# Dynamic filters on one core: pairs of squared filter tiles summed by TensorE alone, its sums of one chunk placed between the taps of the next

## The chip, the cores and the metric

One Trainium2 chip, and of it one core. The metric is the device time of one execution in microseconds (us); lower is better. The kernel before takes 20082.18 us, the median of three runs (20081.55 to 20100.58).

## What is computed

A network of four layers on images of 4 x 64 x 128 x 128, float32. Only the fourth layer, the dynamic filters, is touched:

```python
h = x                                   # x here: the group-normalised input
for _ in range(5):                      # STEPS
    t = gelu(einsum('oc,bchw->bohw', W1, h) + b1)          # exact gelu
    k = einsum('oc,bchw->bohw', W2, t) + b2                # 64 channels x 9 taps
    k = k.reshape(B, C, 9, H, W)
    k = k / (norm(k, axis=2) + 1e-6)                       # over the nine taps
    y = sum(patches(h) * k, axis=2)                        # 3x3 neighbourhood
    h = h + alpha * y
out = x_raw + h
```

So each pixel of each channel makes its own filter of nine taps, which is divided by the root of the sum of its nine squares, and applied to the pixel's neighbours.

## The kernel before, in words

The layers run one after the other. The last one is `dynamic_filters` (L1721 to L2077). The padded image of one batch stands in `df_h`, in both halves of the 128 partitions (64 channels each), one half for the even and one for the odd rows of a chunk. A **chunk** is 8 rows, a tile of 128 partitions x 512 float32. Four chunks are a **group** (c = 0 to 3), four groups an image; 4 batches x 5 steps x 4 groups make 80 groups (`q`) and 320 chunks (`n`).

For one chunk:

- TensorE makes the hidden layer, `hid` (L1823, matmul L1830) with the whole array. ScalarE turns it to `df_t` by a gelu (L1892).
- TensorE makes nine tiles of filters, `tap` (L1832). Taps 0 to 5 (L1840) use 64 rows of the array each, the upper half for even and the lower for odd taps, and can run two at a time. Taps 6 to 8 (L1843) use the whole array. All go through five banks of PSUM (`df_pk`, `BANKS`): tap j waits until square j - 5 has been taken.
- VectorE multiplies each tile of filters, with its bias, by the shifted image (L2056) into `df_pr`; ScalarE squares the same tile (L1902) into `df_sq`, after the product. Both rings hold 15 tiles.
- GpSimd adds squares 0, 2, 4 and 1, 3, 5 (four `add`s, L1954), products 6 and 7 (`singles`, L1959) and squares 6, 7, 8 (two more `add`s).
- TensorE sums products 0 to 5 over the two halves (`sums`, L1851, with the stacked identities `df_pair`), adds product 8 (L1854), both into `df_py`, and sums the two tiles of added squares into `df_pn` (L1861). These matmuls write 64 partitions each, and use 64 columns of the array each, so two can run at a time.
- VectorE joins these with GpSimd's parts (`join`, L1998 and L2001).

The order on TensorE is written out (L1865 to L1876): taps 0 to 5 of chunk n, all sums of chunk n - 1, the hidden matmul of n + 1, taps 6 to 8 of n. On VectorE the join of chunk n - 1 follows product 5 of chunk n (L2063), and on ScalarE the gelu of n + 1 follows square 5.

For a group that is complete, on top: ScalarE takes root, logarithm and exponential of the sums of squares, two instructions each, with three swaps of its function table and a fourth back to the gelu (L1905 to L1921), placed after squares 7 and 8 of chunk 0 and 0 to 3 of chunk 1 of the next group. GpSimd scales (L1965), VectorE checks (L2006) and refines (L2013). Two groups later, in chunk 0, VectorE updates the image (`update`, L2022, after products 0 to 3), or in the last step of a batch writes the output tile (L2028) and adds the raw input (`residual`, L2036, after products 4 to 7); that last case is 16 of the 80 groups. SP's queue copies updated rows between the halves (L1790, L1791) and stores.

Of the kernel before, what the change touches and what calls it, by code (L numbers as in the profile page):

```python
# [18 lines left out]
KK = 9  # L19
# [12 lines left out]
class Steps:  # L32
# [5 lines left out]
    def add(self, ins):  # L38

        ins.then_inc(self.sem, 1)  # L40
        self.n += 1
# [1679 lines left out]
def dynamic_filters(env, ins, x3, out):  # L1721
# [3 lines left out]
    nc = env.nc  # L1725
    CH, GR, R = 4, 4, 8
    N = R // 2 * W
    BANKS, RING = 5, 15
    GROUPS = [(b, step, g) for b in range(B) for step in range(STEPS) for g in range(GR)]
    Q = len(GROUPS)  # L1730
    NC = Q * CH
# [14 lines left out]
    with ExitStack() as m:  # L1746
# [73 lines left out]
        @block.tensor  # L1820
        def _(pe):
            def hid(n):
                b, step, g = GROUPS[n // CH]  # L1823
                if n:
                    pe.wait_ge(active, n)
                if step:
                    pe.wait_ge(moved, CH * updates(b, step, g))
                else:
                    pe.wait_ge(normed, b * GR + g + 1)
                nc.tensor.matmul(p1[:, :], w1[:, :], centre(n), start=True, stop=True).then_inc(hidden, 1)  # L1830

            def tap(n, k):  # L1832
                j = KK * n + k
                if k == 0:
                    pe.wait_ge(active, n + 1)
                if j >= BANKS:
                    pe.wait_ge(squared, j - BANKS + 1)
                if k < 6:
                    p = slice(64 * (k % 2), 64 * (k % 2) + 64)
                    nc.tensor.matmul(pk[:, j % BANKS, :], wp[p, k // 2, :], t[p, n % 2, :], start=True, stop=True,  # L1840
                                     tile_position=(64 * (k % 2), 0)).then_inc(tapped, 1)
                else:
                    nc.tensor.matmul(pk[:, j % BANKS, :], ws[:, k - 6, :], t[:, n % 2, :], start=True, stop=True).then_inc(tapped, 1)  # L1843

            def sums(n):
                pe.wait_ge(product, KK * n + KK)
                if n:
                    pe.wait_ge(yjoined, n)
                for k in range(6):
                    s = k % 2  # L1850
                    nc.tensor.matmul(py[64 * s:64 * s + 64, :], pair[:, :], pr[:, (KK * n + k) % RING, :], start=(k < 2), stop=False,  # L1851
                                     tile_position=(0, 64 * s))
                for s in range(2):
                    last = nc.tensor.matmul(py[64 * s:64 * s + 64, :], env.ident[:, 64 * s:64 * s + 64],  # L1854
                                            pr[:, (KK * n + 8) % RING, :], start=False, stop=True, tile_position=(0, 64 * s))
                last.then_inc(ysummed, 1)
                pe.wait_ge(nadded, 6 * n + 4)
                if n:
                    pe.wait_ge(njoined, n)
                for s in range(2):  # L1860
                    last = nc.tensor.matmul(pn[64 * s:64 * s + 64, :], pair[:, :], sq[:, (KK * n + s) % RING, :], start=True, stop=True,  # L1861
                                            tile_position=(0, 64 * s))
                last.then_inc(nsummed, 1)

            pe.wait_ge(w_in, 64)  # L1865
            hid(0)
            for n in range(NC):
                for k in range(6):
                    tap(n, k)
                if n:  # L1870
                    sums(n - 1)
                if n + 1 < NC:
                    hid(n + 1)
                for k in range(6, KK):
                    tap(n, k)
            sums(NC - 1)  # L1876

        @block.scalar
        def _(act):
# [14 lines left out]
            def square(n, k):  # L1894
                j = KK * n + k
                if k == 0 and n >= 2:
                    act.wait_ge(njoined, n - 1)
                if k == 6 and n:
                    act.wait_ge(nsummed, n)
                act.wait_ge(product, j + 1)  # L1900
                bias = V_B2 + (k // 2 if k < 6 else k - 3)
                nc.scalar.activation(sq[:, j % RING, :], pk[:, j % BANKS, :], ACT.Square, bias=env.vecs[:, bias:bias + 1]  # L1902
                                     ).then_inc(squared, 1)

            def root(q, i):  # L1905
                act.wait_ge(njoined, CH * q + 2 * i + 2)
                n = nr[:, q % 2, 2 * i:2 * i + 2, :]
                nc.scalar.activation(n, n, ACT.Sqrt).then_inc(rooted, 1)  # L1908
# [18 lines left out]
            for n in range(NC):  # L1927
                q, c = n // CH, n % CH
                for k in range(KK):
                    square(n, k)  # L1930
                    if k == 5 and n + 1 < NC:
                        gelu(n + 1)
                    if q and (c, k) in ((0, 7), (0, 8)):
                        root(q - 1, k - 7)
                    if q and (c, k) in ((1, 0), (1, 1)):
                        log(q - 1, k)
                    if q and (c, k) in ((1, 2), (1, 3)):
                        seed(q - 1, k - 2)
                    if q >= 2 and (c, k) == (3, 2):
                        b, step, g = GROUPS[q - 2]  # L1940
                        if step == STEPS - 1 and b + 1 < B:
                            norm(b + 1, g)
# [4 lines left out]
        @block.gpsimd  # L1947
        def _(pool):
            def add(n, into, other, earlier=0):
                pool.wait_ge(squared, KK * n + other + 1)  # L1950
                if earlier:
                    pool.wait_ge(nadded, 6 * n + earlier)
                a = sq[:, (KK * n + into) % RING, :]
                nc.gpsimd.tensor_tensor(a, a, sq[:, (KK * n + other) % RING, :], ALU.add).then_inc(nadded, 1)  # L1954

            def singles(n):
                pool.wait_ge(product, KK * n + 8)
                a = pr[:, (KK * n + 6) % RING, :]
                nc.gpsimd.tensor_tensor(a, a, pr[:, (KK * n + 7) % RING, :], ALU.add).then_inc(sadded, 1)  # L1959

            def scale(q, i):
                pool.wait_ge(seeded, 2 * q + i // 2 + 1)
                pool.wait_ge(yjoined, CH * q + i + 1)
                y = yr[:, q % 2, i, :]
                nc.gpsimd.tensor_tensor(y, y, inv[:, i, :], ALU.mult).then_inc(scaled, 1)  # L1965

            for n in range(NC):
                q, c = n // CH, n % CH
                add(n, 0, 2)
                add(n, 1, 3)  # L1970
                if q and c == 2:
                    scale(q - 1, 1)
                add(n, 0, 4, 1)
                add(n, 1, 5, 2)
                if q and c == 2:
                    scale(q - 1, 2)
                singles(n)
                add(n, 6, 7)
                if q and c == 2:
                    scale(q - 1, 3)  # L1980
                add(n, 6, 8, 5)
                if q and c == 1:
                    scale(q - 1, 0)
            for i in range(CH):
                scale(Q - 1, i)

        @block.vector
        def _(dve):
# [2 lines left out]
            nc.vector.memset(h[64:128, H:H + 1, 1:W + 1], 0.0).then_inc(link, 1)  # L1991
            dve.wait_ge(link, 3)

            def join(n):
                q, c = n // CH, n % CH
                dve.wait_ge(ysummed, n + 1)
                dve.wait_ge(sadded, n + 1)
                nc.vector.tensor_tensor(yr[:, q % 2, c, :], py[:, :], pr[:, (KK * n + 6) % RING, :], ALU.add).then_inc(yjoined, 1)  # L1998
                dve.wait_ge(nsummed, n + 1)
                dve.wait_ge(nadded, 6 * n + 6)  # L2000
                nc.vector.tensor_tensor(nr[:, q % 2, c, :], pn[:, :], sq[:, (KK * n + 6) % RING, :], ALU.add).then_inc(njoined, 1)  # L2001

            def check(q, i):
# [31 lines left out]
                dve.wait_ge(stepout, o + 1)  # L2035
                nc.vector.tensor_tensor(yo[:, i, :], yo[:, i, :], ro[:, i, :], ALU.add).then_inc(o_out, 1)  # L2036

            CHECK = {(1, 6): 0, (1, 8): 1, (2, 1): 2, (2, 3): 3}
            REFINE = {(2, 5): 0, (2, 7): 1, (3, 1): 2, (3, 3): 3}
            dve.wait_ge(env.loaded, env.loads)  # L2040
            nc.vector.tensor_scalar(alpha[:, :], env.vecs[:, V_ALPHA:V_ALPHA + 1], -1.0, None, ALU.mult).then_inc(negated, 1)
            dve.wait_ge(negated, 1)
            for n in range(NC):
                q, c = n // CH, n % CH
                b, step, g = GROUPS[q]
                for k in range(KK):
# [4 lines left out]
                            dve.wait_ge(copied[g - 1], 32 * (b * STEPS + step + 1))  # L2051
                    if k == 6 and c == CH - 1 and g + 1 < GR:
                        dve.wait_ge(copied[g + 1], 32 * (b * STEPS + step + 1))
                    dve.wait_ge(tapped, j + 1)
                    bias = V_B2 + (k // 2 if k < 6 else k - 3)
                    nc.vector.scalar_tensor_tensor(out=rows(pr[:, j % RING, :]), in0=rows(pk[:, j % BANKS, :]),  # L2056
# [3 lines left out]
                        update(q - 2, k)  # L2060
                    if q >= 2 and c == 0 and 4 <= k < 4 + CH and GROUPS[q - 2][1] == STEPS - 1:
                        residual(q - 2, k - 4)
                    if k == 5 and n:  # L2063
                        join(n - 1)
                    if q and (c, k) in CHECK:
                        check(q - 1, CHECK[c, k])
                    if q and (c, k) in REFINE:
                        refine(q - 1, REFINE[c, k])
            join(NC - 1)
            for i in range(CH):  # L2070
                check(Q - 1, i)
                refine(Q - 1, i)
# [149 lines left out]
```

## Time and profile before

| | |
|---|---|
| median of three runs | 20082.18 us |
| the profiled execution | 20080.48 us |
| its span, first to last instruction | 20078.7 us |
| mean granted clock of TensorE, share of full speed | 0.736 |
| TensorE, VectorE, GpSimd, ScalarE busy, of the span | 62%, 52%, 47%, 28% |
| instructions of TensorE's matmuls | 73490 |

The last layer takes the last 4.5 ms. A float32 matmul of 512 columns leaves two records in the trace, one for each half of its passes. "Idle before" in a row is the time for which the engine had stood before it, and "<-" names what ended it. PE is TensorE's matmuls, PEld its weight loads, which can lie under a matmul. A row that ends in xN merges N instructions in a row; its length is from the first one's start to the last one's end.

### The profile page before, as it was taken

To read this page: it belongs to the slowest core of one execution; us is meant where nothing else is said; L and a number is where in the kernel's file an instruction comes from. 1 tells how busy PE (TensorE), PEld (TensorE's weight loads), DVE (VectorE), ACT (ScalarE), POOL (GpSimd) and SP (SyncE) were. 2 spreads that over 40 slices of the span, in tenths; PEclk is the share of its full clock that TensorE was granted. 3 is DMA by queue.
4 is the path that set the end of the run, shared out by engine and by line. 5 is a ranking of instruction groups with operands and counts; after the bars stand their busy time and mean duration, and the time that the engine had idled before them with its cause. 6 is when DMAs were issued, how large, how long until landed. Compare 5 with 4: busy or idle time off the path is not lost. (4 is left out here: it accounts for less than half of the span.)

```text
span 20078.7 us, 217701 instructions
## 1 busy us (share of the span) xinstructions
PE 12353.6 (62%) x73490; PEld 6114.7 (30%) x73490; DVE 10535.6 (52%) x14652; ACT 5526.4 (28%) x7765; POOL 9453.1 (47%) x8026
## 2 busy tenths in 40 slices
PE   5553699999999202333333333333358899999998
PEld 2551366666666101111111111111112333333332
DVE  4557544444444333443443444344422788888887
ACT  1114333333333000000000000000010666666666
POOL 0113100000000106886887788688800787878787
PEclk9999856656666556666666666666679999999999
DMA  4104222222222494335334433533342112121201
GB/s 94 33 21 102 55 38 36 37 38 36 36 37 38 135 195 111 95 95 131 95 95 107 120 95 95 131 96 95 95 86 58 33 22 42 21 42 22 42 19 30
DMA packets 1399772, 1408.47 MB, mean 70 GB/s; under 512 B 771709, under 2 KB 1116045, under 8 KB 1383565
## 3 DMA queue, kind: packets, MB, share of 16 engines
q1 hardware_dynamic: 1106892, 742.84, 18.5%
q0 software_dynamic: 221184, 604.27, 10.4%
q10 hardware_dynamic: 70976, 50.83, 0.8%
q8 instruction: 567, 9.29, 0.2%
q14 instruction: 153, 1.25, 0.0%
HBM read 1036.74 MB, written 276.84 MB: 65 GB/s over the span
## 5 line engine op out<-in xcount | busy, mean ns | idle before, releaser
L1359 POOL DMA_INDIRECT dc_g<-corners,dc_idx x4608 | 5253.7, 1140 | 1326.0 <-issue 1260.9
L1954 POOL TENSOR_TENSOR df_sq<-df_sq 128x512 f32<-128x512 f32 x1920 | 2713.0, 1427 | 1866.6 <-ACT df_sq L1902 1839.5
L1432 PE MATMUL dc_ps<-ident,dc_s 128*128 128x128 f32 x2560 | 674.0, 428 | 4296.9 <-DVE dc_s L1523 4294.8
L1079 POOL TENSOR_TENSOR nz_vp<-nz_vp,nz_den 128x2048 f32<-128x2048 f32 x16 | 105.8, 6610 | 4814.7 <-DMA nz_den<-den_d 4814.7
L1515 DVE TENSOR_TENSOR dc_g<-dc_g,dc_wt 128x2304 f32<-128x2304 f32 x512 | 1308.6, 2556 | 2001.0 <-DMA dc_g<-corners,dc_idx 2000.9
L1902 ACT ACTIVATE df_sq<-df_pk,vecs 128x512 f32<-128x512 f32 x2880 | 1921.1, 685 | 1326.0 <-DVE df_pr L2056 1309.2
L2056 DVE SCALAR_TENSOR_TENSOR df_pr<-df_pk,vecs,df_h 128x512 f32<-128x512 f32 x2880 | 2047.6, 741 | 407.1 <-PE df_pk L1840 264.5
L1432 PEld LDWEIGHTS dc_ps<-ident,dc_s 128*128 128x128 f32 x2560 | 472.0, 218 | 4480.6 <-DVE dc_s L1523 3352.1
L1392 ACT ACTIVATE dc_st<-dc_ps 128x512 f32<-128x512 f32 x640 | 327.0, 607 | 4934.2 <-PE dc_ps L1432 4934.2
L1840 PE MATMUL df_pk<-df_t,df_wp 64*128 64x512 f32 x3840 | 1389.8, 642 | 364.7 <-ACT df_sq L1902 302.1
L916 DVE TENSOR_REDUCE at_mx<-at_pt 128x4 f32<-128x512 f32 x1024 | 707.8, 691 | 1605.4 <-PE at_pt L779 1605.4
L839 PE MATMUL at_prr<-at_a,at_rel 48*128 48x64 bf16 x8192 | 1029.5, 284 | 58.7 <-DMA at_k<-y 58.7
L779 PE MATMUL at_pt<-ident,at_x 128*128 128x128 f32 x4096 | 1053.1, 407 | 0.4 <-DVE at_x L925 0.3
L1851 PE MATMUL df_py<-df_pr,df_pair 128*64 128x512 f32 x3840 | 1025.9, 675 | 1.1 <-DVE df_pr L2056 1.1
L907 DVE SCALAR_TENSOR_TENSOR at_x<-at_pq,hconst,at_x 128x512 f32<-128x512 f32 x1024 | 715.5, 745 | 567.5 <-PE at_pq L759 402.9
L1438 PE MATMUL dc_po<-dc_st,dc_wd 128*64 128x512 f32 x1280 | 864.8, 843 | 92.1 <-ACT dc_st L1392 92.1
L839 PEld LDWEIGHTS at_prr<-at_a,at_rel 48*128 48x128 bf16 x8192 | 825.4, 119 | 307.9 <-ACT at_x L942 171.4
L1843 PE MATMUL df_pk<-df_t,df_ws 128*128 128x512 f32 x1920 | 875.4, 592 | 0.0
L1840 PEld LDWEIGHTS df_pk<-df_t,df_wp 64*128 64x128 f32 x3840 | 495.7, 188 | 1212.6 <-ACT df_sq L1902 816.7
L1234 PE MATMUL cv_po<-cv_xp,cv_w 128*64 x1536 | 682.0, 601 | 275.9 <-DVE cv_xo L1709 168.4
L942 ACT ACTIVATE at_x<-at_prr 128x512 f32<-128x512 f32 x1024 | 610.0, 596 | 869.7 <-PE at_prr L839 869.7
L925 DVE TENSOR_TENSOR at_x<-at_pt,at_x 128x512 f32<-128x512 f32 x1024 | 680.2, 686 | 158.9 <-PE at_pt L797 152.6
(271 smaller groups left out, 19428.1 us busy)
## 6 DMA issues: line engine op xcount, KB each, us to landing
df_h<-df_h SPq DMA_DIRECT2D x160, 512.0 KB, 7.1
dc_g<-corners,dc_idx POOLq DMA_INDIRECT x4608, 2.8
corners<-dc_xt SPq DMA_DIRECT2D x16, 4160.0 KB, 41.5
dc_xp<-x SPq DMA_DIRECT2D x8, 4096.0 KB, 40.8
cv_xp<-x SPq DMA_DIRECT2D x8, 4096.0 KB, 50.0
y<-sp_p SPq DMA_DIRECT2D x128, 192.0 KB, 2.8
y<-sp_p SPq DMA_DIRECT2D x64, 384.0 KB, 4.3
at_a<-y SPq DMA_DIRECT2D x64, 384.0 KB
```

The lines of the kernel that those rows point to most:

```text
L779: last = nc.tensor.transpose(ptt[:, t % 2, 128 * e:128 * e + 128], X[:, s, nh, :], env.ident[:, :])
L839: last = nc.tensor.matmul(prr[:, r % 2, 64 * i:64 * i + 64], rel[:, 127 - p:255 - p], a[0:48, s, :, :].rearrange("c h (n p) -> c (h n) p", ...
L1359: nc.gpsimd.indirect_dma_start(gt[:, r, k, :, :].rearrange("p a c -> p (a c)"), None, image, bass.IndirectOffsetOnAxis(ap=idx[:, s, r, k:k ...
L1432: i = nc.tensor.transpose(ps[:, j, 128 * r:128 * r + 128], sm[:, r % 2, 128 * j:128 * j + 128], env.ident[:, :])
L1438: i = nc.tensor.matmul(po[:, :], wd[:, j, :], stt[:, j, :], start=(j == 0), stop=(j == 4))
L1515: c.run(nc.vector.tensor_tensor(q, q, w, ALU.mult))
L1840: nc.tensor.matmul(pk[:, j % BANKS, :], wp[p, k // 2, :], t[p, n % 2, :], start=True, stop=True, tile_position=(64 * (k % 2), 0)).then_inc ...
L1843: nc.tensor.matmul(pk[:, j % BANKS, :], ws[:, k - 6, :], t[:, n % 2, :], start=True, stop=True).then_inc(tapped, 1)
L1851: nc.tensor.matmul(py[64 * s:64 * s + 64, :], pair[:, :], pr[:, (KK * n + k) % RING, :], start=(k < 2), stop=False, tile_position=(0, 64 * s))
L1902: nc.scalar.activation(sq[:, j % RING, :], pk[:, j % BANKS, :], ACT.Square, bias=env.vecs[:, bias:bias + 1]).then_inc(squared, 1)
L1954: nc.gpsimd.tensor_tensor(a, a, sq[:, (KK * n + other) % RING, :], ALU.add).then_inc(nadded, 1)
L2056: nc.vector.scalar_tensor_tensor(out=rows(pr[:, j % RING, :]), in0=rows(pk[:, j % BANKS, :]), scalar=env.vecs[:, bias:bias + 1], in1=shift ...
```

## The change

GpSimd no longer adds squares 0 to 5; it keeps `singles` and the two adds of squares 6 to 8, in another order (`singles` first). TensorE sums all six squares of the pairs itself, three pairs of matmuls instead of one, accumulated in `df_pn`. `sums` is split into `products(n, i)`, i = 0 to 3, and `squares(n, i)`, i = 0 to 2. In chunk n the squares of n - 1 stand after taps 1, 3 and 5, and the products of n - 1 after taps 6, 7, 8 and once more behind. The rings of products and squares hold 18 tiles, two chunks, and VectorE gets waits before it writes over a product of chunk n - 2. The join is split: products of n - 2 after product 1 of chunk n, squares of n - 1 after product 7. ScalarE loses its wait for the sums of squares, and root, logarithm and exponential are placed one square later; the checks and refinements of VectorE move a little later too.

```diff
-    BANKS, RING = 5, 15
+    BANKS, RING = 5, 18
+    ADDS = 2
...
-            def sums(n):
...
+            def products(n, i):
+                pe.wait_ge(product, KK * n + (2 * i + 2 if i < 3 else KK))
+                if i == 0 and n:
                     pe.wait_ge(yjoined, n)
...
+                for s in range(2):
+                    half = py[64 * s:64 * s + 64, :]
+                    if i < 3:
+                        last = nc.tensor.matmul(half, pair[:, :], pr[:, (KK * n + 2 * i + s) % RING, :], start=(i == 0), stop=False,
+                                                tile_position=(0, 64 * s))
+                    else:
+                        last = nc.tensor.matmul(half, env.ident[:, 64 * s:64 * s + 64], pr[:, (KK * n + 8) % RING, :],
+                                                start=False, stop=True, tile_position=(0, 64 * s))
                 last.then_inc(ysummed, 1)
...
+            def squares(n, i):
+                if i == 0:
+                    pe.wait_ge(squared, KK * n + 2)
+                    if n:
+                        pe.wait_ge(njoined, n)
+                else:
+                    pe.wait_ge(squared, KK * n + 2 * i + 2)
+                for s in range(2):
+                    k = 2 * i + s
+                    last = nc.tensor.matmul(pn[64 * s:64 * s + 64, :], pair[:, :], sq[:, (KK * n + k) % RING, :],
+                                            start=(i == 0), stop=(i == 2), tile_position=(0, 64 * s))
+                if i == 2:
+                    last.then_inc(nsummed, 1)
...
             for n in range(NC):
-                for k in range(6):
-                    tap(n, k)
-                if n:
-                    sums(n - 1)
+                for i in range(3):
+                    tap(n, 2 * i)
+                    tap(n, 2 * i + 1)
+                    if n:
+                        squares(n - 1, i)
                 if n + 1 < NC:
                     hid(n + 1)
                 for k in range(6, KK):
                     tap(n, k)
-            sums(NC - 1)
+                    if n:
+                        products(n - 1, k - 6)
+                if n:
+                    products(n - 1, 3)
...
-                if k == 6 and n:
-                    act.wait_ge(nsummed, n)
...
+                    if q and (c, k) in ((0, 8), (1, 0)):
+                        root(q - 1, c)
+                    if q and (c, k) in ((1, 1), (1, 2)):
+                        log(q - 1, k - 1)
+                    if q and (c, k) in ((1, 3), (1, 4)):
+                        seed(q - 1, k - 3)
...
-                add(n, 0, 2)
-                add(n, 1, 3)
                 if q and c == 2:
                     scale(q - 1, 1)
-                add(n, 0, 4, 1)
-                add(n, 1, 5, 2)
+                singles(n)
                 if q and c == 2:
                     scale(q - 1, 2)
-                singles(n)
                 add(n, 6, 7)
...
-                add(n, 6, 8, 5)
+                add(n, 6, 8, 1)
...
-            CHECK = {(1, 6): 0, (1, 8): 1, (2, 1): 2, (2, 3): 3}
-            REFINE = {(2, 5): 0, (2, 7): 1, (3, 1): 2, (3, 3): 3}
+            CHECK = {(1, 7): 0, (2, 0): 1, (2, 2): 2, (2, 4): 3}
+            REFINE = {(2, 6): 0, (2, 8): 1, (3, 2): 2, (3, 4): 3}
...
+                    if n >= 2 and k in (0, 2, 4, 8):
+                        dve.wait_ge(ysummed, 4 * (n - 2) + min(k // 2, 3) + 1)
+                    if n >= 2 and k == 6:
+                        dve.wait_ge(yjoined, n - 1)
...
-                    if k == 5 and n:
-                        join(n - 1)
+                    if k == 1 and n >= 2:
+                        join_products(n - 2)
+                    if k == 7 and n:
+                        join_squares(n - 1)
```

## Rows read from the trace of the kernel before

**Rows 1.** The page: busy time of each engine, and the second costliest group

```profile
PE 12353.6 (62%) x73490; PEld 6114.7 (30%) x73490; DVE 10535.6 (52%) x14652; ACT 5526.4 (28%) x7765; POOL 9453.1 (47%) x8026
...
L1954 POOL TENSOR_TENSOR df_sq<-df_sq 128x512 f32<-128x512 f32 x1920 | 2713.0, 1427 | 1866.6 <-ACT df_sq L1902 1839.5
```

**Rows 2.** The view of the image's tile: line, engine, count: ns min/median/max, first and last start

```profile
L2056 DVE SCALAR_TENSOR_TENSOR df_pr<-df_pk,vecs,df_h x2880: 729/739/753, 15597.4 to 20027.2; 128x512 f32<-128x512 f32 x192
...
L2022 DVE SCALAR_TENSOR_TENSOR df_h<-df_y,df_alpha,df_h x256: 731/1240/1705, 15696.6 to 19863.6; 128x512 f32<-128x512 f32 x128
```

**Rows 3.** Waits of the whole run: engine, waited for whom: us, times, longest

```profile
POOL df_sq L1954 <- ACT df_sq L1902: 1839.5, 487, 1027.0
...
PEld df_pk L1840 <- ACT df_sq L1902: 816.7, 817, 2.7
```

**Rows 4.** Timeline of TensorE over a group: start us, us, what, records, idle before

```profile
17031.00 2.80 PE L1851 MATMUL df_py<-df_pr,df_pair 128*64 128x512 f32 x12
17033.63 1.03 PE L1854 MATMUL df_py<-df_pr,ident 128*64 128x512 f32 x4
17034.49 1.03 PE L1861 MATMUL df_pn<-df_sq,df_pair 128*64 128x512 f32 x4
17035.45 1.13 PE L1830 MATMUL df_p<-df_h,df_w 128*128 128x512 f32 x2
17036.42 2.73 PE L1843 MATMUL df_pk<-df_t,df_ws 128*128 128x512 f32 x6
17039.08 2.32 PE L1840 MATMUL df_pk<-df_t,df_wp 64*128 64x512 f32 x8
17043.22 1.12 PE L1840 MATMUL df_pk<-df_t,df_wp 64*128 64x512 f32 x2 [1.82 <-ACT df_sq L1902]
17044.75 1.12 PE L1840 MATMUL df_pk<-df_t,df_wp 64*128 64x512 f32 x2 [0.40 <-ACT df_sq L1902]
17045.80 4.49 PE L1851 MATMUL df_py<-df_pr,df_pair 128*64 128x512 f32 x12
...
17051.94 1.13 PE L1830 MATMUL df_p<-df_h,df_w 128*128 128x512 f32 x2
...
17056.45 2.86 PE L1840 MATMUL df_pk<-df_t,df_wp 64*128 64x512 f32 x10 [0.80 <-ACT df_t L1892]
...
17085.76 0.65 PE L1851 MATMUL df_py<-df_pr,df_pair 128*64 128x512 f32 x2
```

**Rows 5.** Views of the lines of hidden and single taps' matmuls, ns min/median/max

```profile
L1830 PE MATMUL df_p<-df_h,df_w x640: 592/698/1193, 15576.8 to 20012.0; 128*128 128x512 f32 x160
...
L1843 PE MATMUL df_pk<-df_t,df_ws x1920: 590/592/697, 15601.0 to 20026.3; 128*128 128x512 f32 x192
```

**Rows 6.** Timeline: weight load of a hidden matmul after sums

```profile
17120.35 0.30 PEld L1830 LDWEIGHTS df_p<-df_h,df_w 128*128 128x128 f32 x2 [0.81 <-issue]
```

**Rows 7.** Timelines: a lone tap and its product; three products and their squares

```profile
17097.98 1.12 PE L1840 MATMUL df_pk<-df_t,df_wp 64*128 64x512 f32 x2 [1.82 <-ACT df_sq L1902]
...
17099.14 0.75 DVE L2056 SCALAR_TENSOR_TENSOR df_pr<-df_pk,vecs,df_h 128x512 f32<-128x512 f32 x1 [1.35 <-PE df_pk L1840]
...
17125.23 2.05 DVE L2056 SCALAR_TENSOR_TENSOR df_pr<-df_pk,vecs,df_h 128x512 f32<-128x512 f32 x3
...
17126.00 2.00 ACT L1902 ACTIVATE df_sq<-df_pk,vecs 128x512 f32<-128x512 f32 x3 [1.29 <-DVE df_pr L2056]
```

**Rows 8.** Timeline of ScalarE: ends of its run of table functions

```profile
17095.00 1.28 ACT L1908 ACT_TABLE_LOAD   x1
...
17110.46 0.69 ACT L1892 ACTIVATE df_t<-df_p,vecs 128x512 f32<-128x512 f32 x1
```

**Rows 9.** Groups of VectorE in the stage: busy us, mean ns, idle before

```profile
L2036 DVE TENSOR_TENSOR df_o<-df_o,df_raw 128x512 f32<-128x512 f32 x64 | 54.5, 859 | 2.3 <-DMA df_raw<-x 2.3
```

**Rows 10.** Stretches: length, busy of PE, PEld, DVE, ACT, POOL, granted clock, DMA

```profile
17101.40:17104.80 3.40, 3.40 (x12) 0.99 (x10) 0.01 (x1) 3.38 (x5) 0.62 (x1) 0.62 0.00 0
```

More of the change, by code:

```diff
@@ L1843, in tap @@
                     nc.tensor.matmul(pk[:, j % BANKS, :], ws[:, k - 6, :], t[:, n % 2, :], start=True, stop=True).then_inc(tapped, 1)
-            def sums(n):
-                pe.wait_ge(product, KK * n + KK)
-                if n:
+            def products(n, i):
+                pe.wait_ge(product, KK * n + (2 * i + 2 if i < 3 else KK))
+                if i == 0 and n:
                     pe.wait_ge(yjoined, n)
-                for k in range(6):
-                    s = k % 2
-                    nc.tensor.matmul(py[64 * s:64 * s + 64, :], pair[:, :], pr[:, (KK * n + k) % RING, :], start=(k < 2), stop=False,
-                                     tile_position=(0, 64 * s))
@@ L1853, in sums @@
                 for s in range(2):
-                    last = nc.tensor.matmul(py[64 * s:64 * s + 64, :], env.ident[:, 64 * s:64 * s + 64],
-                                            pr[:, (KK * n + 8) % RING, :], start=False, stop=True, tile_position=(0, 64 * s))
-                last.then_inc(ysummed, 1)
-                pe.wait_ge(nadded, 6 * n + 4)
-                if n:
-                    pe.wait_ge(njoined, n)
-                for s in range(2):
-                    last = nc.tensor.matmul(pn[64 * s:64 * s + 64, :], pair[:, :], sq[:, (KK * n + s) % RING, :], start=True, stop=True,
-                                            tile_position=(0, 64 * s))
@@ L1863, in sums @@
-                last.then_inc(nsummed, 1)
+                    half = py[64 * s:64 * s + 64, :]
[5 more added lines that the diff above has]
+                                                start=False, stop=True, tile_position=(0, 64 * s))
@@ L1867, in _ @@
             for n in range(NC):
-                for k in range(6):
-                    tap(n, k)
-                if n:
-                    sums(n - 1)
+                for i in range(3):
[3 more added lines that the diff above has]
+                        squares(n - 1, i)
                 if n + 1 < NC:
@@ L1875, in _ @@
                     tap(n, k)
-            sums(NC - 1)
+                    if n:
+                        products(n - 1, k - 6)
+                if n:
+                    products(n - 1, 3)
+            for i in range(3):
+                squares(NC - 1, i)
+            for i in range(4):
+                products(NC - 1, i)
         @block.scalar
@@ L1932, in _ @@
                         gelu(n + 1)
[L1933 to L1938, printed above, removed]
+                    if q and (c, k) in ((0, 8), (1, 0)):
[4 more added lines that the diff above has]
+                        seed(q - 1, k - 3)
                     if q >= 2 and (c, k) == (3, 2):
@@ L1951, in add @@
                 if earlier:
-                    pool.wait_ge(nadded, 6 * n + earlier)
+                    pool.wait_ge(nadded, ADDS * n + earlier)
                 a = sq[:, (KK * n + into) % RING, :]
@@ L1992, in _, with join_products, join_squares @@
             dve.wait_ge(link, 3)
-            def join(n):
+            def join_products(n):
                 q, c = n // CH, n % CH
-                dve.wait_ge(ysummed, n + 1)
+                dve.wait_ge(ysummed, 4 * n + 4)
                 dve.wait_ge(sadded, n + 1)
                 nc.vector.tensor_tensor(yr[:, q % 2, c, :], py[:, :], pr[:, (KK * n + 6) % RING, :], ALU.add).then_inc(yjoined, 1)
+            def join_squares(n):
+                q, c = n // CH, n % CH
                 dve.wait_ge(nsummed, n + 1)
-                dve.wait_ge(nadded, 6 * n + 6)
+                dve.wait_ge(nadded, ADDS * n + ADDS)
                 nc.vector.tensor_tensor(nr[:, q % 2, c, :], pn[:, :], sq[:, (KK * n + 6) % RING, :], ALU.add).then_inc(njoined, 1)
@@ L2068, in _ @@
                         refine(q - 1, REFINE[c, k])
-            join(NC - 1)
+            join_products(NC - 2)
+            join_squares(NC - 1)
+            join_products(NC - 1)
             for i in range(CH):
```

## The prediction

> **What bounds the kernel now.** The page first: it gives each engine's busy time and names the costliest groups; GpSimd's additions of squares at L1954 stand second, 1920 of them at 1.43 us [rows 1]. Then the tile of the image: the 2880 products run from 15597.4 to 20027.2 us, 4430 us for 320 chunks of nine, 13.85 us a chunk [rows 2]. Only this stage is touched.
>
> Then the waits. GpSimd sat 1839.5 us waiting for ScalarE's squares, 1027.0 of them in one wait that began ahead of the stage, so 812 in it: it is ahead of its work; TensorE's weight loads sat 816.7 us until a square freed a bank of products' filters [rows 3]. So the additions that the change takes away are not what the stage waits for. What it waits for is a ring: tap, product, square, bank free, next tap.
>
> Then TensorE's own timeline over one group of four chunks, from the sums of one group's chunk 0 to the same place in the next: 17031.00 to 17085.76, 54.76 us [rows 4]. 80 such groups make 4381 us; the other 49 us are the 16 groups in which the residual is added too. Within it the reader is to see three things. (a) Where TensorE runs unhindered, every matmul costs two records 0.429 us apart, 0.858 us, and two taps on the two row halves, or two sums on the two column halves, share one such slot: the pair of sums at 17033.63 to 17034.49 is 0.86. I call 0.858 a slot. (b) One chunk in four is long: 17035.45 to 17051.94 from one hidden matmul to the next, 16.5 us, because ScalarE swaps tables and TensorE idles 1.82 and 0.40 us. (c) A slot that follows another partition of the array costs more.
>
> **What a change of partition costs.** From sums (column halves) to the hidden matmul (whole array): 17034.49 to 17035.45, 0.96, and then 0.97 to the first single tap, where slots are 0.86. Three single taps and the change to row halves: 17036.42 to 17039.08, 2.66 against 3 x 0.858 = 2.57 [rows 4]. The first record after such a change lasts 698 ns (median of the line) and not 592 [rows 5]: its weight load, two records of 0.30 us in all, starts only together with the matmul, 0.81 us after the previous one [rows 6], where otherwise it lies under the matmul before. So 0.09 of gap and 0.11 of unhidden load: 0.20 us into whole or row halves. Into the column halves a load has 64 columns: one tap and the change take 17044.75 to 17045.80 = 1.05, and of that 0.11 is the tap's own late load, 0.86 its slot, so the gap is 0.08 to 0.09; the three pairs after it at 17031.00 take 2.63 for 2.57, so 0.05 to 0.06 of load. 0.14 us.
>
> **The change, part by part.**
> TensorE before: 3 tap pairs, 3 single taps, the hidden matmul, 4 pairs for products, 1 for squares, 12 slots = 10.30 us, and 3 changes (0.14 + 0.20 + 0.20), 10.84 us of 13.85.
> TensorE after: 2 pairs of squares more, 14 slots = 12.01 us. The order is now tap pair, squares, tap pair, squares, tap pair, squares, hidden and tap 6, products, tap 7, products, tap 8, two pairs of products: 12 changes, 6 into column halves (0.84 to 0.85) and 6 into the others (1.20): 2.05 us. Sum **14.06 us a chunk**, already 0.21 over what a chunk takes now. All of it is on the path, since nothing can shorten TensorE's own queue.
> Waits inside it. In the steady state I find none: a bank is free again 1.16 (tap to product) + 0.77 (product to square) + 0.69 (square) = 2.6 us after its tap [rows 7], and five taps further on there are at least 4.1 us of TensorE's queue (two tap pairs and two pairs of squares with changes). VectorE in chunk 0: 9 products and 2 joins at 0.66 apart (three products in 2.05 us, one alone 0.74, [rows 2, 7]) and 4 updates at about 1.2 [rows 2]: product 8 may start 1.16 + 10 x 0.66 + 4 x 1.2 = 12.6 us after the first tap, and its tap is ready at 11.15 + 1.16 = 12.3. Chunk 2 with 3 checks and 2 refinements fills VectorE to some 13.5 of 14.06. Both just fit.
> ScalarE, the one stall left. Its run from the first table load to the end of the gelu is 17095.00 to 17111.15, 16.15 us without a gap [rows 8]. Root, logarithm and exponential move one square later, so one square of 0.6 less lies between: 15.6. It begins when the square of tap 8 of chunk 0 is done: tap 8's start + 2.6. The gelu ends at tap 8 + 18.2 and the first tap of chunk 2 needs it. TensorE would arrive there at tap 8 + 2.9 (its slot, two pairs, changes) + 14.06 = 17.0. Stall 1.3, taken as 1.35. Taps 5 to 8 of chunk 1 need squares that end before TensorE reaches them (tap 8: square 3, at about + 12 us against 13.9).
> A group: 4 x 14.06 + 1.35 = **57.6 us** against 54.76: 80 x 2.84 = +227 us.
> The 16 groups with residuals: four additions of 0.86 us [rows 9] lie ahead of product 8 of chunk 0 on VectorE, so the run of ScalarE starts later. Before, this costs 49/16 = 3.1 us a group. After, I take 2.5 (updates meet GpSimd less), but TensorE then idles near 4 us in one piece, and the clock should fall as it does today after 1.82 + 0.40 of idling: + 1.7. So 4.2 for 3.1: +16 us.
> GpSimd: 4 of 8 additions a chunk go. Their gain lies on VectorE: an update lasts 731 ns alone and 1240 at the median, while a product that reads PSUM stays at 739 [rows 2]. But VectorE is not what the next tap waits for, so I cost it at nothing; if TensorE were not the cover it would be worth up to 0.5 us for each of 12 operations a group. The joins' separate places, the ring of 18 and VectorE's five new waits: each waits for matmuls at least most of a chunk old, nothing. The wait of ScalarE for the sums of squares goes, nothing. DMAs: none moves, SP's queue sees the same updates. End of the stage: three pairs more before the last joins, less GpSimd work behind; within 2 us, -1 taken.
> The granted clock now falls once a group: sums that take 2.80 at full clock (2.4 GHz) take 4.49 at 17045.80, a clock of 0.62 over 17101.40 to 17104.80 in the next group, where 0.5 would be 1.2 GHz throughout [rows 4, 10]. These 1.7 us are inside the 54.76 of now. I take it that 1.35 us of idling once a group leaves the clock up: the 0.80 us at 17056.45 does, 1.82 + 0.40 doesn't [rows 4]. It is between them, and this is the widest uncertainty.
> Changes from column halves to row halves and from the whole array to column halves appear in no row of before. Bounds: nothing, or 0.20 and 0.14 as their mirror images. If nothing, 2 x 0.20 + 3 x 0.14 = 0.82 go, a chunk is 13.24, the stall grows to about 3.0 because ScalarE's run starts with VectorE's product 8 and not with the tap, and a group is 56.0: +99 us and so still slower. I take the mirror images. The Trainium skill, "TensorEngine Tiling (Array Packing)", section Key Properties, says that a change of tiling mode drains the engine, not merely a change of tile; by that all twelve are paid, and the sum would be the one above. The rows agree for the three kinds that occur.
>
> Sum: profiled execution 20080.5 (span 20078.7 and 1.8 around it) + 227 + 16 - 1 = 20322; the median of the runs shown is 1.7 above the profiled one. **20320 us.**
>
> **Rivals.**
> 1. The clock falls in every group. For: 1.35 us of idling is nearer to 1.82 than to nothing; against: it is one short piece, and elsewhere TensorE is full. 64 more groups x 1.7 = +109: **20430**.
> 2. No stall at the gelu (ScalarE's run shorter or earlier than I count) or the unseen changes cheap: 320 x 14.06 = 4499 against 4430, +70, or the +99 above: **20150 to 20190**.
> 3. Faster: the interleaved changes are hidden, since weight loads could be drawn ahead between waits. For: nothing in the rows except that the unseen kinds are unseen; against: all 320 hidden matmuls show it. Then TensorE needs 12.01 a chunk and VectorE with ScalarE set the time: product 8 of chunk 0 at about 10.6 with updates at 0.73, gelu 17.0 later, the next two chunks at 12: 27.7 + 24 = 51.8 a group, 80 x -3.0 = -235: **19845**. It decides once a change costs under 0.05 us. With VectorE not relieved, the group is 55.2 and the kernel the same within 40 us.
> 4. Nothing to see: the change is off the path altogether. It can't be for TensorE's order, so this is small: **20080**.
>
> **How the numbers follow.** Forecast 0.58, rival 1 0.22, rival 2 0.09, rival 3 0.06, rival 4 with the half-relieved case 0.05. 0.2% is 40 us, about what a measurement of this kernel tells from no change. Slower 0.58 + 0.22 + 0.09 = 0.89; faster 0.06; same 0.05. Range: 20130 (the low end of rival 2) to 20450 (rival 1 and 20 us); outside it lie 0.11 below and perhaps 0.08 above, for stalls of chunk 2 where VectorE just fits.
>
> **What would show it.** TensorE busy all but 1 to 2 us a group; hidden matmuls 14.0 to 14.1 us apart in chunks 2, 3 and 0, and some 15.4 for the one that holds the gelu's stall; first records after a change at 698 and 643 ns, 12 times a chunk; updates on VectorE at 0.73 to 1.1 us; GpSimd's busy share in the stage about halved; the clock full in groups without residual. Hidden matmuls 12 to 13 us apart would prove the price of a change wrong; long gaps before squares or products would show a wait that I missed.

## The result

The changed kernel takes 20282.06 us, the median of four runs (20270.30 to 20296.69), against 20081.86 us (four runs): ratio 1.0098, 95% interval 1.0081 to 1.0116. It is slower by 200 us; forecast was 240 us, 20320, in a range from 20130 to 20450. The profiled execution took 20271.4 us, its span is 20269.5, and 191 us of the difference to the span of before lie between the first and the last product of the stage: 4621.3 us for 4429.8 [rows 2].

The page and the view of the image's tile (columns as in [rows 1, 2]), changed kernel:

```profile
PE 12789.9 (63%) x76050; PEld 5870.8 (29%) x76050; DVE 10144.9 (50%) x14652; ACT 5525.8 (27%) x7765; POOL 7624.2 (38%) x6746
...
L2074 DVE SCALAR_TENSOR_TENSOR df_pr<-df_pk,vecs,df_h x2880: 733/747/753, 15597.6 to 20218.9; 128x512 f32<-128x512 f32 x192
...
L2036 DVE SCALAR_TENSOR_TENSOR df_h<-df_y,df_alpha,df_h x256: 740/744/751, 15705.9 to 20053.8; 128x512 f32<-128x512 f32 x128
```

GpSimd works 1829 us less, VectorE 391 us less, and the kernel is slower: the time that they had been busy was not the bound. TensorE's timeline, one chunk and the stall (columns as in [rows 4]):

```profile
17303.21 1.13 PE L1831 MATMUL df_p<-df_h,df_w 128*128 128x512 f32 x2
17304.18 1.02 PE L1844 MATMUL df_pk<-df_t,df_ws 128*128 128x512 f32 x2
17305.13 1.08 PE L1853 MATMUL df_py<-df_pr,df_pair 128*64 128x512 f32 x4
17306.14 1.13 PE L1844 MATMUL df_pk<-df_t,df_ws 128*128 128x512 f32 x2
17307.19 1.08 PE L1853 MATMUL df_py<-df_pr,df_pair 128*64 128x512 f32 x4
17308.20 1.13 PE L1844 MATMUL df_pk<-df_t,df_ws 128*128 128x512 f32 x2
17309.26 1.08 PE L1853 MATMUL df_py<-df_pr,df_pair 128*64 128x512 f32 x4
17310.17 1.03 PE L1856 MATMUL df_py<-df_pr,ident 128*64 128x512 f32 x4
17311.12 1.13 PE L1841 MATMUL df_pk<-df_t,df_wp 64*128 64x512 f32 x4
17312.18 1.08 PE L1869 MATMUL df_pn<-df_sq,df_pair 128*64 128x512 f32 x4
17313.19 1.13 PE L1841 MATMUL df_pk<-df_t,df_wp 64*128 64x512 f32 x4
...
17317.33 1.13 PE L1831 MATMUL df_p<-df_h,df_w 128*128 128x512 f32 x2
...
17331.45 1.13 PE L1831 MATMUL df_p<-df_h,df_w 128*128 128x512 f32 x2
...
17345.57 1.13 PE L1831 MATMUL df_p<-df_h,df_w 128*128 128x512 f32 x2
...
17354.86 1.13 PE L1841 MATMUL df_pk<-df_t,df_wp 64*128 64x512 f32 x4 [1.30 <-ACT df_t L1909]
...
17361.06 1.13 PE L1831 MATMUL df_p<-df_h,df_w 128*128 128x512 f32 x2
```

Read the distances of the starts. The hidden matmuls stand 14.12, 14.12, 14.12 and 15.49 us apart, 57.85 a group. No row between carries an idle time but the one of 1.30 us, for the gelu. Between two changes of partition a slot takes 1.05 to 1.06 us for taps (17306.14 to 17307.19) and 1.01 for sums (17305.13 to 17306.14). The products at 17309.26 follow a change but have none behind them: they take 0.91, the plain 0.86 and 0.05 of a weight load that was not hidden. Waits views of the stage, the kernel before first and then the changed one, show that VectorE now waits for TensorE's taps far longer:

```profile
DVE df_pr L2056 <- PE df_pk L1840: 232.4, 259, 1.9
```

```profile
DVE df_pr L2074 <- PE df_pk L1841: 752.3, 407, 3.4
DVE df_pr L2074 <- PE df_pk L1844: 684.3, 693, 1.6
```

### The profile page after: what moved, and what is told of

It reads as the page before. It is cut to its first block and busy times, and to the rows that moved or that the text cites. A ratio compares the mean times of both kernels' runs of the same rounds, so it can differ in the third digit from the quotient of the medians.

```text
span 20269.5 us, 221854 instructions
## 1 busy us (share of the span) xinstructions
PE 12789.9 (63%) x76050; PEld 5870.8 (29%) x76050; DVE 10144.9 (50%) x14652; ACT 5525.8 (27%) x7765; POOL 7624.2 (38%) x6746
## 5 line engine op out<-in xcount | busy, mean ns | idle before, releaser
L2074 DVE SCALAR_TENSOR_TENSOR df_pr<-df_pk,vecs,df_h 128x512 f32<-128x512 f32 x2880 | 2097.7, 746 | 1478.7 <-PE df_pk L1841 784.6
L1974 POOL TENSOR_TENSOR df_pr<-df_pr 128x512 f32<-128x512 f32 x320 | 411.0, 1284 | 3546.7 <-DVE df_pr L2074 3546.7
L1841 PE MATMUL df_pk<-df_t,df_wp 64*128 64x512 f32 x3840 | 1085.3, 642 | 124.2 <-ACT df_t L1909 124.2
L1844 PE MATMUL df_pk<-df_t,df_ws 128*128 128x512 f32 x1920 | 1046.0, 626 | 0.0
L1869 PE MATMUL df_pn<-df_sq,df_pair 128*64 128x512 f32 x3840 | 1035.1, 617 | 0.0
L1969 POOL TENSOR_TENSOR df_sq<-df_sq 128x512 f32<-128x512 f32 x640 | 867.7, 1356 | 410.1 <-ACT df_sq L1917 397.3
```

## The experiments

Eight kernels in two sets, each set on one chip with runs of the kernel before beside it. On the first chip that took 20080.59 us (13 runs), on the second 20195.65 (13 runs). In the four kernels traced on the second chip the stage begins at 15665 to 15716 us, and at 15564 to 15574 in all the others. The kernel before has no trace there, so that its 115 us lie ahead of the stage is inferred from those four. Across sets I therefore compare the stage, first to last product, and TensorE's chunks and groups, which come from the hidden matmuls' starts. In the table, slots and changes are counted per chunk, the chunk is the distance of two hidden matmuls (one number: that of the chunks without a stall), and a group is four chunks.

| kernel | slots, changes | chunk | group | stage | median, against before on its chip |
|---|---|---|---|---|---|
| before | 12, 3 | 12.0 to 16.5 | 54.76 | 4429.8 | |
| changed | 14, 12 | 14.12 | 57.85 | 4621.3 | 1.0098 [1.0081, 1.0116] |
| e1 blocks | 14, 5 | 12.92 | 54.53 | 4375.3 | 20032.96, 0.9976 [0.9966, 0.9986] |
| e2 products together | 14, 8 | 13.42 | 55.76 | 4474.9 | 20135.18 (one run) |
| e3 functions earlier | 14, 12 | 14.12 | 56.91 | 4542.4 | 20206.08, 1.0065 [1.0048, 1.0082] |
| e4 squares alone in before's order | 14, 3 | 13.66 to 19.4 | 61.4 | 4899.8 | 20557.62 (one run) |
| e5 GpSimd adds | 12, 8 | 12.82 to 15.48 | 54.5 | 4404.6 | 20188.63 (one run) |
| e6 e1 and functions earlier | 14, 5 | 12.92 | 53.84 or 55.49 | 4361.3 | 20112.69 (one run) |
| e8 e1 and functions spread | 14, 5 | 12.92 | 52.34 | 4179.4 | 19963.18, 0.9882 [0.9865, 0.9898] |
| e9 e8 and GpSimd adds | 12, 5 | 12.6 to 14.2 | 54.68 | 4395.4 | 20170.37, 0.9989 [0.9980, 0.9999] |

**e1_blocks and e2_products_together: the price of a change.** e1, on the changed kernel:

```diff
-                for i in range(3):
-                    tap(n, 2 * i)
-                    tap(n, 2 * i + 1)
-                    if n:
+                for k in range(4):
+                    tap(n, k)
+                if n:
+                    for i in range(3):
                         squares(n - 1, i)
+                tap(n, 4)
+                tap(n, 5)
...
                 for k in range(6, KK):
                     tap(n, k)
-                    if n:
-                        products(n - 1, k - 6)
                 if n:
-                    products(n - 1, 3)
+                    for i in range(4):
+                        products(n - 1, i)
```

> The changed kernel with another order on TensorE alone: taps 0 to 3, all three pairs of squares, taps 4 and 5, the hidden matmul, taps 6 to 8, all four pairs of products. The same 14 slots and the same waits, but 5 changes of the array's partition instead of 12. Theory (TensorE's queue with priced changes is the bound): 12.01 + 2 x 0.14 + 3 x 0.20 = 12.89, with the 0.06 that the changed kernel showed over the estimate 12.95 us a chunk; ScalarE's run then ends about 1.6 us after TensorE's arrival, 53.4 us a group, about 19915 us in all. Rival (the interleaving is free and two more slots with new waits make the time): TensorE's chunk stays at 14.1 and the time at 20280; or the longer blocks starve VectorE and the time is above 20280.

e2 has the second half of that edit alone.

> The changed kernel with all four pairs of products behind tap 8, squares as they are: 8 changes instead of 12. Theory: 12.01 + 4 x 0.14 + 4 x 0.20 + 0.06 = 13.43 us a chunk, a stall of about 0.6 at the gelu, 54.3 us a group, about 19990 us. Rival (changes are free): hidden matmuls stay 14.12 us apart, 20280 us.

The timelines of TensorE, e1 and then e2:

```profile
17309.77 1.13 PE L1831 MATMUL df_p<-df_h,df_w 128*128 128x512 f32 x2
...
17313.08 1.13 PE L1844 MATMUL df_pk<-df_t,df_ws 128*128 128x512 f32 x2 [0.46 <-ACT df_sq L1918]
...
17319.55 2.28 PE L1841 MATMUL df_pk<-df_t,df_wp 64*128 64x512 f32 x8 [1.76 <-ACT df_t L1910]
...
17325.54 1.13 PE L1831 MATMUL df_p<-df_h,df_w 128*128 128x512 f32 x2
...
17338.46 1.13 PE L1831 MATMUL df_p<-df_h,df_w 128*128 128x512 f32 x2
```

```profile
17324.52 1.13 PE L1831 MATMUL df_p<-df_h,df_w 128*128 128x512 f32 x2
...
17337.94 1.13 PE L1831 MATMUL df_p<-df_h,df_w 128*128 128x512 f32 x2
...
17351.37 1.13 PE L1831 MATMUL df_p<-df_h,df_w 128*128 128x512 f32 x2
...
17366.85 1.13 PE L1831 MATMUL df_p<-df_h,df_w 128*128 128x512 f32 x2
```

With the same 14 slots the chunk is 14.12, 13.42 and 12.92 us for 12, 8 and 5 changes: 0.175 us for each of the first four taken away, 0.167 for each of the next three. Continued to no change that is 12.92 - 5 x 0.17 = 12.07, the 14 slots of 0.86. Both chunks were forecast to 0.03 us, and the rival that the interleaving is free is out. The totals were not: 20033 for 19915, 20135 for 19990, mainly because the stall was 2.85 us (15.77 - 12.92) and 2.06, not 1.6 and 0.6; over 80 groups that is 100 of the 118 us, and 117 of the 145. ScalarE's timeline of e1 shows why:

```profile
17303.01 1.28 ACT L1924 ACT_TABLE_LOAD   x1
...
17306.17 0.69 ACT L1918 ACTIVATE df_sq<-df_pk,vecs 128x512 f32<-128x512 f32 x1 [0.81 <-DVE df_pr L2075]
...
17318.81 0.69 ACT L1910 ACTIVATE df_t<-df_p,vecs 128x512 f32<-128x512 f32 x1
```

The run, from the first table load to the end of the gelu, is 16.5 us and not 15.6: it now has a hole of 0.81, since the first product of the next chunk comes only after the whole block of products. In e2 the same hole is 1.32 us. I had priced the run as solid.

**e3_functions_earlier: the stall.** Root, logarithm and exponential back at (0, 7), (0, 8), (1, 0) to (1, 3), nothing else.

> The changed kernel with root, logarithm and exponential back at the places of the kernel before (after squares 7 and 8 of chunk 0, 0 to 3 of chunk 1), nothing else. Theory (ScalarE's run holds up one chunk in four by 1.37 us): the run starts one tap earlier, about 2 us, and has one square more in it, so its gelu ends before TensorE arrives; all chunks 14.12, 56.5 us a group, 20282 - 110 = about 20170 us. Rival (that chunk is long for another reason, VectorE's checks or the clock): one chunk in four stays at 15.5 us and the time at 20280.

```profile
17323.67 1.13 PE L1831 MATMUL df_p<-df_h,df_w 128*128 128x512 f32 x2
...
17332.01 1.13 PE L1841 MATMUL df_pk<-df_t,df_wp 64*128 64x512 f32 x4 [0.35 <-ACT df_t L1909]
...
17338.22 1.13 PE L1831 MATMUL df_p<-df_h,df_w 128*128 128x512 f32 x2
...
17352.34 1.13 PE L1831 MATMUL df_p<-df_h,df_w 128*128 128x512 f32 x2
```

14.55 for 15.49, so 0.94 of the 1.37 us went, 79 us of the stage, and 0.35 us of waiting for the gelu stay; I had expected all of it to go (20206 us for about 20170). The long chunk is ScalarE's run, and moving the functions one square later cost the change about 75 us (80 x 0.94). It is more than a third of all that the change lost.

**e4_before_squares_alone: the squares without the new order.** The kernel before; the sums block gets three pairs of squares, GpSimd's four adds go:

```diff
-                pe.wait_ge(nadded, 6 * n + 4)
+                pe.wait_ge(squared, KK * n + 6)
...
-                add(n, 0, 2)
-                add(n, 1, 3)
...
-                add(n, 0, 4, 1)
-                add(n, 1, 5, 2)
```

> The kernel before with one part of the change: TensorE sums all six squares of the pairs itself, in the one block of sums, GpSimd's four additions gone; rings, joins and order as before, so 3 changes. Theory (VectorE's join and with it the next tap wait for the whole block of sums, so the two slots of 0.86 come on top of the ring, partly paid back by updates that GpSimd no longer delays): some 58 us a group, 20280 to 20400 us. Rival (TensorE has 3 us to spare in each chunk, so the slots hide, and VectorE's shorter updates win): 20080 or below.

```profile
17304.50 1.13 PE L1830 MATMUL df_p<-df_h,df_w 128*128 128x512 f32 x2
...
17318.16 1.13 PE L1830 MATMUL df_p<-df_h,df_w 128*128 128x512 f32 x2
...
17329.04 5.16 PE L1851 MATMUL df_py<-df_pr,df_pair 128*64 128x512 f32 x12
...
17337.56 1.13 PE L1830 MATMUL df_p<-df_h,df_w 128*128 128x512 f32 x2
...
17352.27 1.13 PE L1830 MATMUL df_p<-df_h,df_w 128*128 128x512 f32 x2
```

61.4 us a group, 6.7 more than before, where I had expected some 58 and at most 20400 us in all. The sum is close to the 4 x 1.72 us of the two slots, but it is not spread evenly: the chunks grew by 1.7, 2.9, 1.0 and 1.05 us. So the slots don't hide, though TensorE itself has 3 us to spare in a chunk: with the block between tap 5 and the join, the ring of tap, product and square stands on them. In the two that grew by 1.0, VectorE's shorter updates (916 ns at the median) may have paid back a part; that was argued, not tested. In the long chunk part of the growth is the clock, which is lowered there as before: the block of products takes 5.16 us for 4.49. How the rest of the 2.9 arises was not taken apart. The changed kernel, with the new order, rings, joins and places of the functions together, does the same work in 4621.3 us of stage and not 4899.8, and the rival that the squares hide is out.

**e5_gpsimd_adds: the new order without the squares.** `ADDS = 6`, GpSimd's order of before, and `squares` sums one pair of added tiles, at i = 2.

> The changed kernel with GpSimd adding squares 0 to 5 again and TensorE summing one pair of tiles, as in the kernel before; the interleaved order, the rings, the split joins and the places of the functions stay. TensorE: 12 slots and 8 changes, 10.30 + 1.36 = 11.7 us a chunk. Theory (the changed kernel is bound by TensorE's queue): the time falls below 20282, until VectorE's updates, delayed by GpSimd again, and ScalarE's run set it: 29.6 us for chunks 0 and 1, 13.6 and 12.0 for the others, 55.3 a group, about 20080 us. Rival (the new waits or rings cost the time, not the slots and changes): it stays near 20280.

```profile
17310.24 1.13 PE L1831 MATMUL df_p<-df_h,df_w 128*128 128x512 f32 x2
...
17323.06 1.13 PE L1831 MATMUL df_p<-df_h,df_w 128*128 128x512 f32 x2
...
17336.44 1.13 PE L1831 MATMUL df_p<-df_h,df_w 128*128 128x512 f32 x2
...
17351.92 1.13 PE L1831 MATMUL df_p<-df_h,df_w 128*128 128x512 f32 x2
```

The stage falls from 4621.3 to 4404.6 us, and the kernel equals the one before on its chip (20188.6 for 20195.7, one run): as forecast for TensorE's queue as the bound, and against waits, rings or joins as the cause, which e5 keeps. Two slots and four changes less are 2.4 us a chunk, 9.6 a group, and only 3.4 of them came back: once the queue is shorter, waits set the time. Even the quiet chunks take 12.82 us, where the queue alone was priced at 11.7. VectorE's updates, at a median of 1091 ns, are again among what can hold it up.

**e6, e8, e9: what the order could give.** e6 is e1 with e3's places. e8 spreads ScalarE's functions over two gelus:

```diff
-                    if q and (c, k) in ((1, 1), (1, 2)):
-                        log(q - 1, k - 1)
-                    if q and (c, k) in ((1, 3), (1, 4)):
-                        seed(q - 1, k - 3)
+                    if q and (c, k) in ((1, 6), (1, 7)):
+                        log(q - 1, k - 6)
+                    if q and (c, k) in ((1, 8), (2, 0)):
+                        seed(q - 1, c - 1)
...
+            CHECK = {(2, 2): 0, (2, 4): 1, (2, 6): 2, (2, 8): 3}
+            REFINE = {(3, 0): 0, (3, 2): 1, (3, 4): 2, (3, 6): 3}
```

with `scale` 0 and 1 in chunk 2 and 2 and 3 at the start of chunk 3. e9 is e8 with GpSimd adding as in e5.

> e1_blocks with root, logarithm and exponential one square earlier, as in e3. In e1 the chunk with the gelu's stall took 15.77 us against 12.92. Theory (ScalarE's run is what makes it long): the stall falls from 2.85 to some 1.8 us a group, 20033 - 80 = 19950 us. Rival (another wait): no change.

> e1_blocks with ScalarE's functions spread over two gelus: roots after square 8 of chunk 0 and 0 of chunk 1, table back for the gelu, logarithms after squares 6 and 7 and exponentials after 8 of chunk 1 and 0 of chunk 2, with one table load more in a group; scaling, checks and refinements later to match (last refinement in chunk 3). Theory: no chunk waits for a gelu, four chunks of 12.92 make 51.7 us a group against 54.54, 20033 - 80 x 2.85 = about 19805 us. Rival (ScalarE as a whole or VectorE's crowded chunks 2 and 3 take the gain): 19950 to 20030.

> e8 with GpSimd adding squares 0 to 5 again and one pair of squares on TensorE: 12 slots and 5 changes, 11.2 us a chunk. If TensorE's two slots are the whole cost of moving the squares, the time falls by 80 x 4 x 1.72 = 550 us from e8's. Theory: it falls by much less, since VectorE's updates, checks and refinements (1.24 us and not 0.73 while GpSimd works) then fill three chunks of four to 12.3 to 12.6 us: 49 to 50 us a group, 19600 to 19700 us. Rival (GpSimd's eight to ten additions of 1.4 us a chunk bind): 13.5 to 14 us a chunk, no better than e8.

TensorE in e8, and one stretch of it (columns as in [rows 10]):

```profile
17303.49 1.13 PE L1831 MATMUL df_p<-df_h,df_w 128*128 128x512 f32 x2
...
17316.41 1.13 PE L1831 MATMUL df_p<-df_h,df_w 128*128 128x512 f32 x2
...
17329.99 1.13 PE L1831 MATMUL df_p<-df_h,df_w 128*128 128x512 f32 x2
...
17342.91 1.13 PE L1831 MATMUL df_p<-df_h,df_w 128*128 128x512 f32 x2
...
17355.83 1.13 PE L1831 MATMUL df_p<-df_h,df_w 128*128 128x512 f32 x2
```

```profile
17000.00:18000.00 1000.00, 1000.00 (x3667) 333.33 (x3664) 743.33 (x1085) 732.61 (x980) 409.28 (x304) 1.00 0.17 33
```

e8 beats both kernels: 0.9882 of before, TensorE busy without a gap, 52.34 us a group where 51.7 was forecast; 0.66 us remain in one chunk. Against e1 the stage is 196 us shorter (forecast 228). The 19963 us fall into the range that I had written down for the rival, but all those figures were meant for the first chip; by the stage and by the group it is the theory that came. This is the bound by 14 slots and 5 changes.

e6 fell short of its forecast: 14 us of stage and not 80. Its chunk with the stall has one piece of idling:

```profile
17352.70 1.13 PE L1844 MATMUL df_pk<-df_t,df_ws 128*128 128x512 f32 x2 [1.82 <-ACT df_sq L1918]
```

Its ordinary groups are 53.84 or 55.49 us, and the trace's record of the granted clock tells them apart without an exception: of 78 whole groups, 30 hold one stretch of lowered clock, and these are the ones that are about 1.65 us longer. That is what the lowered clock cost before, too (4.49 - 2.80 = 1.69), where all 78 groups have such a stretch; the changed kernel and e8 have none. So the earlier places did shorten e6's ordinary group by 0.7 us, and the clock took most of it back.

e9 did not come near its forecast of 49 to 50 us a group. Its two slots less gained nothing: e8's order ran 216 us of stage slower with GpSimd adding. TensorE's records and one line of the waits view:

```profile
17303.66 2.07 PE L1831 MATMUL df_p<-df_h,df_w 128*128 128x512 f32 x2
...
17333.63 1.13 PE L1844 MATMUL df_pk<-df_t,df_ws 128*128 128x512 f32 x2 [1.15 <-ACT df_sq L1915]
```

```profile
POOL df_sq L1967 <- ACT df_sq L1915: 1956.3, 554, 1027.2
```

The hidden matmul at 17303.66 runs at the lowered clock (2.07 us for 1.13), and the tap at 17333.63 waits for a square. The group of 54.68 us, 13.7 a chunk, is what I had written down for the rival, that GpSimd's additions bind. The waits speak against that as the whole cause: GpSimd itself stood idle for ScalarE's squares, 1956.3 us, 1027.2 of them in one wait that began ahead of the stage. Updates on VectorE are back at a median of 1234 ns. The clock is a part and not all: 73 of 78 groups have a stretch of lowered clock, and the three ordinary ones without it take 53.5 us, still more than e8's 52.34. How much each of these holds e9 back was not taken apart.

## Why the prediction was right, and where its sizes were off

- **The bound and the price of a change** were right: TensorE's queue, 14.06 us forecast, 14.12 measured, and 0.17 us a change as the mean of 0.14 and 0.20. The two kinds of change that no row of before showed cost what their mirror images do: the products at 17305.13, after a single tap, take 1.01 us to the next start, as the squares at 17312.18 do after a tap pair, and the tap pair at 17311.12, after sums, 1.06. In the bound for these kinds being free I had counted too few: the new order has three changes from column halves to row halves in a chunk and not two, so 1.02 us and not 0.82 would have gone. The forecast does not use that figure.
- **The stall** was right in size (1.35 forecast, 1.37 measured), in its parts (ScalarE's run 15.6 us forecast, 17339.17 to 17354.81 = 15.64 measured) and in cause (e3 took 0.94 of it away).
- **GpSimd's additions at nothing**: right for this kernel, whose queue on TensorE is the bound, but no run takes the additions away without giving TensorE their work. It does not hold in every order: with e8's order the kernel is 216 us of stage faster without the additions on GpSimd, though TensorE has two slots more.
- **The 16 groups with residuals were mis-sized.** I gave them 4.2 us above the others: 2.5 for a later run and 1.7 for a fallen clock. Measured is 0.28: one such group has 18967.11 to 18982.88 = 15.77 where the others have 15.49.

```profile
18967.11 1.13 PE L1831 MATMUL df_p<-df_h,df_w 128*128 128x512 f32 x2
...
18982.88 1.13 PE L1831 MATMUL df_p<-df_h,df_w 128*128 128x512 f32 x2
```

  The mis-sized term is "updates at about 1.2 us" and additions of 0.86 in the place of VectorE's product 8: the output's updates take 744 ns at the median, the residual's additions 683, so that all of them nearly fit in front of tap 8. Those groups are 3.5 us longer than the others in the kernel before (58.27 for 54.74 us; I had inferred 3.1). And with 1.58 us of idling in one piece the clock did not fall either. Against the forecast that is 16 x (4.2 - 0.28) = 63 us. With the ordinary groups 0.25 us longer than forecast (57.85 for 57.6, +20 us) this makes 240 - 63 + 20 = 197, for 191 to 200 measured. The two misses have opposite signs, so the total is somewhat closer than its parts.
- **The clock** (rival 1) did not fall. Over 17000 to 18000 us the granted clock is 1.00, the 2.4 GHz level, with one piece of idling of 1.30 us a group; in the kernel before it was 0.95. That 1.30 us would leave the clock up was taken between 0.80 and 1.82 + 0.40 and not worked out, so here the forecast was partly lucky.

```profile
17000.00:18000.00 1000.00, 975.20 (x3313) 251.43 (x3312) 689.83 (x982) 649.86 (x870) 367.89 (x277) 1.00 0.15 30
```

- **Rival 3**, the changes hidden, is out by e1 and e2; rival 2 by the 1.30 us row (no stall) and by the 1.01 and 1.06 us above (unseen changes cheap); rival 4, nothing to see, by the ratio of 1.0098.

## What to carry to other kernels

Before interleaving matmuls of different shape on the array, count the changes of partition and price one from the trace (here 0.17 us, a fifth of a float32 slot); blocks of one shape, split only where a bank ring would run dry, keep the overlap for half the price. Work taken from an engine that is not what the others wait for gains nothing while another queue is the bound, and the same work on an engine that then has no slack costs its full length. Ask it anew for every order: in e8's, the additions on GpSimd (e9) cost more than two slots on TensorE do. Once one queue is full, look for the single run on another engine that still stops it, and spread that, as e8 does.

## What the runs showed of the hardware that I had not expected

- VectorE's updates (two operands in SBUF) went from a median of 1240 ns to 744, with a maximum of 751, though GpSimd still works 37% of the stretch above. GpSimd's first addition of a chunk now waits for product 7 (3546.7 us of waiting at L1974 over the run, 1028.9 of them one wait ahead of the stage), so it works late in a chunk, and the updates stand early: laid side by side in the trace, none of the 256 updates meets an instruction of GpSimd. In the kernel before, the 64 updates that meet none take 737 ns at the median and those covered wholly by one about 1380. What counts is when the two meet, not how busy they are. The checks, later in the chunk, still take 1066 ns on average.
- In e1 one piece of idling of 1.76 us and one of 0.46 in a group left the clock up in all 65 ordinary groups, where 1.82 and 0.40 us with lone taps around them lowered it in each group of the kernel before; in e6 one piece of 1.82 us lowered it in some groups and not in others. The length of the longest gap alone doesn't tell. Each fall cost these kernels the same: the groups with one are about 1.65 us longer than their like in e1, e2 and e6.
- The same kernel took 115 us more on a second chip, as far as the other traces show ahead of the stage studied; without runs of before beside each set, e8's gain would have been read as half its size.
